# A recurrent scan whose state is kept in PSUM by VectorE and copied to SBUF by ScalarE, with another layout of the products with r

## What is computed

```python
def step(S, ins):
    r_t, w_t, k_t, v_t, a_t, b_t = ins
    Sa = jnp.einsum('bhvk,bhk->bhv', S, a_t)
    S = S * jnp.exp(w_t)[:, :, None, :] + Sa[..., None] * b_t[:, :, None, :] + v_t[..., None] * k_t[:, :, None, :]
    o = jnp.einsum('bhvk,bhk->bhv', S, r_t)
    return (S, o)
_, o = jax.lax.scan(step, S0, (tm(r), tm(w), tm(k), tm(v), tm(a), tm(b)))
```

## Time and profile before

| | us |
|---|---|
| median of 3 timed runs | 3199.55 (3199.02 to 3200.14) |
| the profiled execution, its own time | 3204.26 |
| its span, first to last instruction | 3202.10 |
| scan, from 87.5 to 360.0 of the span | 272.5 |
| mean granted TensorE clock, share of full | 0.917 |

### The profile page before, as it was taken

One profiled execution on the slowest core, in us unless ns is written; L12 is line 12 of the kernel. 1 busy time (PEld: TensorE's weight loads), 2 busy tenths in 40 slices (PEclk: granted clock), 3 DMA queues, 4 the chain that ended last, 5 costly groups with the idle time before them and its releaser, 6 DMA issues. The chain is left out here.

```text
span 3202.1 us, 62703 instructions
## 1 busy us (share of the span) xinstructions
PE 2742.3 (86%) x23863; PEld 1858.1 (58%) x23924; DVE 2221.3 (69%) x3616; ACT 1336.8 (42%) x1913; POOL 1893.7 (59%) x1955
## 2 busy tenths in 40 slices
PE   5788759677899999999978999999634789999998
PEld 2454535544577777777755666666410456666666
DVE  5888544636577676676668788887586488888774
ACT  2000003232566666666623555455422134555454
POOL 0899400000787877878736788887300157888885
PEclk8889859888899999999989999999866799999999
DMA  1000000001111010010010000000000100000000
GB/s 38 1 1 1 1 19 1 11 20 50 24 25 25 18 28 22 22 28 17 14 52 1 2 1 2 2 2 2 17 0 0 52 1 2 1 2 2 1 1 15
DMA packets 31170, 41.72 MB, mean 13 GB/s; under 512 B 10344, under 2 KB 17896, under 8 KB 30880
## 3 DMA queue, kind: packets, MB, share of 16 engines
q1 hardware_dynamic: 30880, 37.76, 4.3%
HBM read 19.91 MB, written 1.05 MB: 7 GB/s over the span
## 5 line engine op out<-in xcount | busy, mean ns | idle before, releaser
L1367 POOL TENSOR_TENSOR at_p_lo<-at_p_t 128x512 bf16<-128x512 f32 x512 | 522.9, 1040 | 159.0 <-ACT at_p_t L1337 127.2
L1873 PE MATMUL banks<-g_w,normed_t 128*128 128x320 f32 x1536 | 500.9, 454 | 30.0 <-DVE g_scratch L2161 29.9
L1337 ACT COPY g_p_t<-banks 128x512 f32<-128x512 f32 x512 | 287.6, 588 | 400.4 <-PE banks L1308 399.5
L2161 DVE TENSOR_TENSOR g_scratch<-banks,g_gate 128x640 f32<-128x640 f32 x384 | 314.4, 822 | 194.0 <-PE banks L1873 191.0
L1355 DVE TENSOR_REDUCE at_negmax<-banks 128x1 f32<-128x1024 f32 x256 | 301.6, 1220 | 211.3 <-PE banks L1286 211.3
L1367 POOL TENSOR_TENSOR g_p_lo<-g_p_t 128x512 bf16<-128x512 f32 x256 | 266.4, 1044 | 150.9 <-ACT g_p_t L1337 128.8
L1873 PEld LDWEIGHTS banks<-g_w,normed_t 128*128 128x128 f32 x1536 | 268.9, 194 | 120.8 <-DVE g_scratch L2161 47.1
L1355 DVE TENSOR_REDUCE g_negmax<-banks 128x1 f32<-128x1024 f32 x256 | 310.5, 1218 | 30.7 <-PE banks L1286 30.4
L1350 ACT ACTIVATE g_p<-banks,g_negmax 128x1024 f32<-128x1024 f32 x256 | 286.0, 1117 | 98.4 <-DVE g_negmax L1355 90.8
L1337 ACT COPY at_p_t<-banks 128x512 f32<-128x512 f32 x384 | 211.9, 587 | 255.9 <-PE banks L1308 250.8
L1308 PEld LDWEIGHTS banks<-identity,g_p 128*128 128x128 f32 x2048 | 235.8, 142 | 139.3 <-issue 117.2
(11 more groups left out here) (389 smaller groups left out, 5943.3 us busy)
## 6 DMA issues: line engine op xcount, KB each, us to landing
at_swapped<-at_crossed SPq DMA_DIRECT2D x256, 64.0 KB, 2.0
g_w<-in_ex_w SPq DMA_DIRECT2D x2, 2880.0 KB, 11.6
f_w<-in_W SPq DMA_DIRECT2D x2, 1024.0 KB, 5.5
at_rope<-in_rope SPq DMA_DIRECT2D x1, 2048.0 KB, 9.6
g_w<-in_ex_w SPq DMA_DIRECT2D x2, 960.0 KB, 5.4
out<-residual SPq DMA_DIRECT2D x1, 1024.0 KB, 5.1
at_w<-in_at_w SPq DMA_DIRECT2D x1, 768.0 KB, 4.6
rw_weights<-in_rw_w SPq DMA_DIRECT2D x1, 512.0 KB, 3.7
```

What stands on the lines that cost most here:

```text
L1337: self.nc.scalar.copy(self.pt[:, j % self.deep, h, g * CHUNK:(g + 1) * CHUNK], self.core.ps[self.home(n)]).then_inc(self.pt_copied, 1)
L1367: self.nc.gpsimd.tensor_tensor(self.p_lo[:, j % self.deep, h, part], self.pt[:, j % self.deep, h, part], self.pt_hi[:, j % self.deep, h, p ...
L1873: nc.tensor.matmul(out[:, 0:ED], core.xt[:, at:at + P], w[:, kind * H + tile // (T * BATCH) * 2 + h, :], start=True, stop=True).then_inc(p ...
L2161: v.tensor_tensor(qk_product[:, tile % 2, kind] if kind < 2 else v_product[:, tile % 2], core.banks[:, bank:bank + 2, 0:ED].rearrange("p h ...
```

## The change

- `yr` gets the layout `[P, 2, ROWS, COLS, BLOCK]`: the step within the block is innermost. Lines 425 and 428 then write elements with 1 KB between rows and 32 B between columns; line 294 reads a contiguous row.
- `ub` is gone. VectorE writes the product with b into the second half of bank b (`lot(b, 1)`), the sum into bank 6 + b (`lot(6 + b, s % 2)`), and makes the product with a from there.
- ScalarE copies the sum to `state` in SBUF, one copy for each step and b (`copy_state`), after `y_ready` tells that the product with a has read it; the new semaphore `x_copied` counts the copies.
- GpSimd's three kinds of instruction wait on `x_copied` in place of `x_ready`.
- ScalarE's copy of the first output moves behind step 4's state copies, that of the second to the end of the block.

```diff
-        yr = sb("yr", [P, 2, BLOCK, COLS, ROWS])
+        yr = sb("yr", [P, 2, ROWS, COLS, BLOCK])
...
-        ya, ub, x1 = sb("ya", [P, 2, PER, ROWS]), sb("ub", [P, 2, PER, ROWS]), sb("x1", [P, 2, PER, ROWS])
+        ya, x1 = sb("ya", [P, 2, PER, ROWS]), sb("x1", [P, 2, PER, ROWS])
...
+        lot = lambda bank, i: core.ps[bank][:, 256 * i:256 * i + 256].rearrange("p (c r) -> p c r", r=ROWS)
...
-                ins = mm(core.ps[4 + row // K][:, 0:256], pick[:, row % K, :], yr[:, i, :, :, row].rearrange("p s c -> p c s"),
+                ins = mm(core.ps[4 + row // K][:, 0:256], pick[:, row % K, :], yr[:, i, row],
...
+            act.wait_ge(y_ready, 2)
+            act.sem_inc(x_copied, 2)
+
+            def copy_outputs(q, i):
+                act.wait_ge(o_full, q * 2 + i + 5)
...
+            def copy_state(n, s, b):
+
+                act.wait_ge(y_ready, n * 2 + b + 3)
+                nc.scalar.copy(state[:, s % 2, b * PER:(b + 1) * PER], lot(6 + b, s % 2)).then_inc(x_copied, 1)
 
             with act.Fori(0, STEPS // BLOCK) as q:
-                copy_outputs(q)
-            copy_outputs(STEPS // BLOCK)
+                for s in range(BLOCK):
+                    for b in range(BATCH):
+                        copy_state(q * BLOCK + s, s, b)
+                    if s == 4:
+                        copy_outputs(q, 0)
+                copy_outputs(q, 1)
+            for i in range(2):
+                copy_outputs(STEPS // BLOCK, i)
...
-                            pool.wait_ge(x_ready, n * 2 + b + 1)
+                            pool.wait_ge(x_copied, n * 2 + b + 1)
...
-                        g.tensor_tensor(yr[:, j, slot], before, seq["r"][:, :, bass.ds(n, 1)].to_broadcast([P, COLS, ROWS]),
-                                        ALU.mult).then_inc(yr_ready, 1)
...
+                        g.tensor_tensor(yr[:, j, :, :, slot].rearrange("p r c -> p c r"), before,
+                                        seq["r"][:, :, bass.ds(n, 1)].to_broadcast([P, COLS, ROWS]), ALU.mult).then_inc(yr_ready, 1)
+            pool.wait_ge(x_copied, STEPS * 2 + 2)
...
-                            step(v.tensor_tensor(ub[:, b], core.ps[b][:, 0:256].rearrange("p (c r) -> p c r", r=ROWS),
-                                                 seq["b"][:, mine, bass.ds(n, 1)].to_broadcast([P, PER, ROWS]), ALU.mult))
+                            step(v.tensor_tensor(lot(b, 1), lot(b, 0), seq["b"][:, mine, bass.ds(n, 1)].to_broadcast([P, PER, ROWS]), ALU.mult))
                             dve.wait_ge(x1_ready, n * 2 + b + 1)
-                            v.tensor_tensor(state[:, s % 2, mine], ub[:, b], x1[:, b], ALU.add).then_inc(x_ready, 1)
-                            dve.wait_ge(x_ready, n * 2 + b + 3)
-                            times_a(n + 1, b, state[:, s % 2])
+                            v.tensor_tensor(lot(6 + b, s % 2), lot(b, 1), x1[:, b], ALU.add).then_inc(x_ready, 1)
+                            dve.wait_ge(x_ready, n * 2 + b + 1)
+                            times_a(n + 1, b, lot(6 + b, s % 2))
```

More of the change, by code:

```diff
@@ L219, in rwkv_stage @@
         inv = sb("inv", [P, CHUNK])
-        flat_yr = yr[:].rearrange("p i s c r -> p (i s c r)")
+        flat_yr = yr[:].rearrange("p i r c s -> p (i r c s)")
         square = flat_yr[:, 0:2048].rearrange("p (t c) -> p t c", c=P)
@@ L232, in rwkv_stage @@
         y_ready, u_full, x1_ready, x_ready = sem("y_ready"), sem("u_full"), sem("x1_ready"), sem("x_ready")
+        x_copied = sem("x_copied")
         yr_ready, v_full, kv_ready, o_full, o_copied = (sem(n) for n in ("yr_ready", "v_full", "kv_ready", "o_full", "o_copied"))
@@ L388, in _ @@
             act.sem_inc(o_copied, 2)
[L390 to L393, removed]
-            with act.Fori(0, STEPS // BLOCK) as q:
-                copy_outputs(q)
-            copy_outputs(STEPS // BLOCK)
+            act.wait_ge(y_ready, 2)
+            act.sem_inc(x_copied, 2)
+            def copy_outputs(q, i):
+                act.wait_ge(o_full, q * 2 + i + 5)
+                nc.scalar.copy((o, yc)[i][:, :, bass.ds(q * BLOCK, BLOCK)],
+                               core.ps[4 + i][:, 0:256].rearrange("p (c s) -> p c s", s=BLOCK)).then_inc(o_copied, 1)
+            def copy_state(n, s, b):
+                act.wait_ge(y_ready, n * 2 + b + 3)
+                nc.scalar.copy(state[:, s % 2, b * PER:(b + 1) * PER], lot(6 + b, s % 2)).then_inc(x_copied, 1)
+            with act.Fori(0, STEPS // BLOCK) as q:
+                for s in range(BLOCK):
[6 more added lines that the diff above has]
+                copy_outputs(STEPS // BLOCK, i)
             for m in range(COLS // 4):
@@ L424, in _ @@
                         j, slot = (i, s - 1) if s else (1 - i, BLOCK - 1)
-                        g.tensor_tensor(yr[:, j, slot], before, seq["r"][:, :, bass.ds(n, 1)].to_broadcast([P, COLS, ROWS]),
-                                        ALU.mult).then_inc(yr_ready, 1)
-            pool.wait_ge(x_ready, STEPS * 2 + 2)
-            g.tensor_tensor(yr[:, 1, BLOCK - 1], state[:, 1], seq["r"][:, :, STEPS:STEPS + 1].to_broadcast([P, COLS, ROWS]),
-                            ALU.mult).then_inc(yr_ready, 1)
+                        g.tensor_tensor(yr[:, j, :, :, slot].rearrange("p r c -> p c r"), before,
+                                        seq["r"][:, :, bass.ds(n, 1)].to_broadcast([P, COLS, ROWS]), ALU.mult).then_inc(yr_ready, 1)
+            pool.wait_ge(x_copied, STEPS * 2 + 2)
+            g.tensor_tensor(yr[:, 1, :, :, BLOCK - 1].rearrange("p r c -> p c r"), state[:, 1],
+                            seq["r"][:, :, STEPS:STEPS + 1].to_broadcast([P, COLS, ROWS]), ALU.mult).then_inc(yr_ready, 1)
         @block.vector
@@ L477, in times_a @@
                 mine = slice(b * PER, (b + 1) * PER)
-                v.tensor_tensor(ya[:, b], src[:, mine], seq["a"][:, mine, bass.ds(n, 1)].to_broadcast([P, PER, ROWS]),
+                v.tensor_tensor(ya[:, b], src, seq["a"][:, mine, bass.ds(n, 1)].to_broadcast([P, PER, ROWS]),
                                 ALU.mult).then_inc(y_ready, 1)
@@ L484, in _ @@
             for b in range(BATCH):
-                times_a(0, b, state[:, 1])
-            dve.sem_inc(x_ready, 2)
+                times_a(0, b, state[:, 1, b * PER:(b + 1) * PER])
             with step.loop(STEPS // BLOCK // 2, 2 * BLOCK * 2) as qq:
```

## The result

| us | before | after |
|---|---|---|
| median of the timed runs | 3199.33 (3199.02 to 3200.14, 4 runs) | 3155.88 (3151.40 to 3158.86, 4 runs) |
| ratio after / before, 95% interval | | 0.9863, 0.9846 to 0.9880 |
| the profiled execution, its own time | 3204.26 | 3151.4 |
| its span | 3202.10 | 3149.6 |
| mean granted TensorE clock | 0.917 | 0.923 |

The change is 43.5 us faster.

The account below looks back on a forecast made before the run. GpSimd's work was taken to bound the scan at 4.025 us a step; 64 steps at 3.54 save 31.0, plus 2.0 at edges, less 1.1 at the end: 31.9 off 3199.55 gives 3168 us, range 3161 to 3200.

Parts of the forecast that it names:

- The collisions go: VectorE's sum and a product, reading PSUM, no longer collide with GpSimd; GpSimd's step sums to 3.43 us against 4.025.
- Rival E: Collisions stay, since one SBUF input still passes; time about 3205 us; chance 0.06 together with the large half of D.
- The strided write: GpSimd's r product, writing with a 1 KB step, takes 1.18 us, which makes the step 3.52.
- A: Strided write costs something in between, r product 1.35 to 1.6 us; at 1.56 the time is 3191 us; chance 0.15.
- B: The strided memset's extra adds fully to the r product, 1.68 us; step 4.02, gain eaten, time 3198 us; chance 0.10.
- C: GpSimd's strided writes run in turn with its reads, 1.01 us more per r product; time 3225 us; chance 0.11.
- ScalarE's hop has cover: ScalarE's state copy in the loop to GpSimd takes 2.90 us, under 3.52; second batch row has 0.4 us of cover.
- VectorE is under GpSimd's step: VectorE's own step, kv included, is 3.04 us on average, under GpSimd's 3.52.
- rival D: VectorE becomes the bound, PSUM writes costing 0.27 us each; 3173 or 3205 us; large half and E together 0.06.
- contiguous rows gain zero: TensorE's products take 2.3 us a step, under 3.52, so its reading of contiguous rows gains zero.
- The edges: At block edges the kv wait shortens, gaining 2.0 us; ScalarE's branch is about covered; the scan's end loses 1.1.
- the 0.02 of reserve: Added to GpSimd's 3.52 us step for steps with three outputs or a kv, giving 3.54.

Follow-up runs that it names:

- e3: Changed kernel with the sum written to SBUF directly and no ScalarE copy, so the a product has two SBUF inputs; 3174.71 us, ratio 0.9930.
- e5: Changed kernel with one extra unused VectorE product a step, both inputs in SBUF; 3170.15 us, ratio 0.9914.
- e6: Changed kernel with one extra unused VectorE product a step, its first input in PSUM; 3158.24 us, ratio 0.9877.
- e1: Changed kernel with the old layout of yr, so GpSimd writes contiguously and TensorE reads with a step; 3166.86 us, ratio 0.9905.
- e4: Changed kernel with a second ScalarE copy of the same size ahead of each state copy; 3158.08 us, ratio 0.9878.
- e9: Changed kernel with GpSimd's kv wait behind the block's first w product, and VectorE making the second batch row's r product every other step; 3152.08 us, ratio 0.9864.
- e8: Changed kernel with the r product of the second batch row left out; 3145.57 us, ratio 0.9838.
- e2: Kernel before with the new layout of yr alone; 3191.28 us, ratio 0.9983.

## Why the prediction was right or wrong, point by point

**1. The collisions go: right.** The w product's median is 641 ns and its maximum 654; the addition has 519 on average; the sum 432. With the working of the prediction, but the measured r product (1.107 instead of 1.09), the step is 3.43 plus 0.017, and that is the 3.447 measured. e3, e5 and e6 show the cause: the spread goes with the second SBUF input. Rival E is excluded.

**2. The strided write: the term was mis-sized.** The prediction took 1.18 us; 1.107 was measured, and e1 with contiguous writes has 1.096. The step was worked out as if the write ran at the strided memset's 1.98 ns an element and was the slower side. It costs 0.011 us for 512 elements. The 0.07 us too much, in 64 steps, are 4.7 us of the missing gain. Rivals A, B and C fall with it. So does carrying the rule for reads from the Trainium skill's page "GPSIMD Engine Reference" over to writes, which would have added 0.43 us: the runs show 0.011. Line 435 still takes 519 ns where the prediction's estimate for a plain one is 398; that the read with a step is the reason fits, but no run changed it.

**3. ScalarE's hop has cover: right.** The prediction had 0.4 us. e4's 0.37 cost nothing. How much more would fit is not shown: e9 added 0.60 to one hop in four and gained nothing, but VectorE was nearly full in it. In after GpSimd waits for a state copy only 8 times, 4.4 us in all, behind the edges.

**4. VectorE is under GpSimd's step, and writing PSUM costs nothing: right within 11 ns.** The b product, whose output is now in the bank that it reads, went from 413 ns to 424; the sum with both in PSUM has 432. The 0.27 of rival D isn't there. In e8 VectorE's own work comes out at 3.03 a step, the prediction's 3.04, and the step falls no further than 3.13.

**5. TensorE, "contiguous rows gain zero": this is the step that failed.** The prediction read "six outputs take 2.74 us", "0.46 each". The x6 are instructions, and each f32 product here is two of them: line 296 has 288 instructions for 16 x 9 = 144 outputs. So it was three outputs of 0.9 us, and TensorE's step was not 2.3 us but about 3.0 (two products of line 312 and one of line 287 at 0.43, two outputs at 0.86; this is an estimate from lengths back to back, and from 99 to 119 us of before the profile has TensorE busy for 17.27 of 20, which is 3.5 a step). Inside the scan that was still under 4.025, so the error did no harm there: e2 shows 0.7 us for the layout in the scan. But the prediction never asked where the same 32 instructions stand without cover. Behind the scan they are the whole path, 14.18 us, and they became 7.17. A line for it is missing in the sum. It also hid that with the old layout TensorE would have come close to the new step of 3.45: e1 lost 2.6 us of scan by it.

**6. The edges: the waits right, the sum not.** The kv wait is 1.16 us (forecast 1.2); a mid edge costs 1.12 over a plain step where it cost 1.42, so four give 1.2 us. A loop edge costs 2.29, 2.45 and 2.49 over two plain steps (the first from 141.27 to 150.45; forecast 2.0), and behind the first and the third another step is late, by 0.73 (153.88 to 158.06) and 0.78. Together that is 8.7 us where the three cost 7.3, so they lose 1.5 us instead of gaining 1.2. GpSimd waits for ScalarE's copy in all of these places, so ScalarE's branch, "about covered", isn't quite. In the late step, though, the copy is late because TensorE is. It had stood idle for 3.63 us at the edge, its clock was down at 0.50, and six output instructions took 2.77 us ahead of the product that VectorE needs:

```profile
149.74 2.77 PE L296 MATMUL banks<-rw_yr,rw_pick 128*128 128x256 f32 x6
...
153.44 0.43 DVE L509 TENSOR_TENSOR banks<-banks,rw_b 128x256 f32<-128x256 f32 x1 [1.25 <-PE banks L314]
...
154.01 1.46 PE L296 MATMUL banks<-rw_yr,rw_pick 128*128 128x256 f32 x6
```

Behind the second edge the clock came back sooner (0.59 over the same six), VectorE waited 0.54 us, and no step was late. The prediction had no clock in its edges. The last r product comes 1.81 us behind the one before it, 1.63 before; against the plain steps of 3.447 and 4.025 this loses 0.76 (forecast 1.1).

The sum again with the measured terms: the step's 4.025 less 3.447, times 64, is 37.0; the measured 35.5 leave a loss of 1.5 for the edges and the end (the terms above give 1.1: 1.2 won at the mid edges, 1.5 lost at the loop edges, 0.8 at the end); and 7.0 behind the scan make 42.5, where the medians say 43.5. The prediction's 31.9 lacked 6 from the step (0.07 for the r product and the 0.02 of reserve, which wasn't needed) and 7 from the tail, and had some 2.4 too much at edges and end. The bottom of the range was set as "the stride is free and the edges give a little more (36 us)". The stride was all but free, the edges gave less and not more, and the scan's 35.5 stayed within it; the stretch behind the scan, a tail that the sum lacked, took the time out of the range: 3155.88 plus 7.0 is 3162.9. That the tail gave the whole 7.0 is partly luck with the clock. The change run again, where it gave 5.3, gained 37.5 us (3159.95 against 3197.44).

## What to carry to other kernels

When a change touches the operand of an instruction, list every place where that instruction runs: a gain hidden inside a loop is paid out in full where the same line runs alone behind it. Check what a count in the profile counts (here two instructions for each f32 product) before a duration is divided by it. And where VectorE and GpSimd stretch each other's instructions, look for the VectorE instructions with two SBUF inputs: putting one input in PSUM, with an idle ScalarE to carry the copy for GpSimd, brought both to their minimum.

## What the runs showed of the hardware that was not expected

TensorE reading its moving f32 rows with 2 KB from element to element took as long at a granted clock of 0.50 as at 1.00. Two rows of before, with the old layout, the first at a clock of 0.50, the second, that of the earlier trace rows, at 1.00:

```profile
93.72 2.78 PE L294 MATMUL banks<-rw_yr,rw_pick 128*128 128x256 f32 x6
...
199.89 2.74 PE L294 MATMUL banks<-rw_yr,rw_pick 128*128 128x256 f32 x6
```

The same six with contiguous rows, in the two rows of after under point 6 above, took 2.77 us at 0.50 and 1.46 at 1.00. In the long row behind the scan that is about 0.43 us an instruction with the step and 0.22 without it at 1.00, the 2.4 GHz level. So the step hid half of the engine's speed, and it cost nothing more where the clock was down at 0.50, the 1.2 GHz level. Second, a GpSimd write with 1 KB between rows and 32 B between columns costs 0.011 us in a product of 512 elements with two inputs, though a memset with 20 B from element to element took 603 ns where contiguous ones point to 308. The runs do not tell whether that is due to the size of the step or to the two reads beside it.
